# Attention and quantised feed-forward on one core: transposing DMAs ahead of the store, and another tail

## The chip, the cores and the metric

The kernel runs on one core of one Trainium2 chip. The metric is the time of one execution on the device, in microseconds (us); lower is better. Besides the plain runs there is one execution that the hardware profiler recorded; all rows below are from it.

## The reference

For each of 8 batches of 512 rows of 512 numbers, cross attention of the normalised rows over a context, with a dropout mask, a residual, then a feed-forward whose activations are rounded to integers row by row:

```
scores = layernorm(x) @ ctx.T / 0.72
attn   = softmax(scores) * mask
x      = x + (attn @ ctx + bias) @ W
h      = layernorm(x)
scale  = max(|h|) / 127                 (per row, at least 1e-6 / 127)
q      = clip(round(h / scale), -128, 127)
out    = x + (q @ Wq.T) * scale * wscale + ffn_bias
```

## The kernel before

**Tiles.** The 4096 rows are 32 tiles of 128 rows, four to a batch. Per tile TensorE multiplies three times with float32 numbers split in a high and a low part (`product3`, 12 matmuls of 512 columns): context times W (`ctx_times_w`, into ps_vw, a batch ahead), scores (ps_scores), and probabilities times that product (`attend`, ps_attn). `turn_probs` transposes the probabilities (ps_pt) between, and `feed_forward` multiplies the integers, transposed (xq_t), with the weights (ps_ffn, four matmuls in bfloat16).

**Engines.** ScalarE makes the high parts, the exponential, the normalised rows (x_norm), the centred rows (x1_neg) and their rounding to integers (x1_int, in two steps, L840 and L852). VectorE makes the low parts, maxima, statistics, residual (x1) and the output's scaling (`scale_ffn`); it turns blocks of 32x32 of the context (ct_raw) and of the normalised rows (xt_raw), which the DMA has laid out from DRAM (ctx_in; x_blocks from norm_rows, where SyncE stores x_norm first). GpSimd has the rest: context's low part, small factors, and the additions of the bias and of the output.

**Order.** Each engine has a hand-written list: steps d, in a head (tiles 0 to 3), a loop of three rounds of eight steps (tiles 4 to 27), and a tail (28 to 31, base `TAIL` = 28). Engines wait for each other by semaphores only. The code is written for a step `d`: in a step, work for tile d (scores, probabilities), d - 1 (`attend`, residual, centring), d - 2 (feed-forward) and d + 1 to d + 4 (loads, context) stands in a row. SyncE issues every DMA of the kernel, and an issue that waits holds up all that follow it. In a step its list is: context blocks for two tiles (every other step), the four loads of x_blocks for tile d + 1 (`load_rows`), x for d + 4, mask for d + 2, the store of x_norm for d + 2 (`store_rows`), the output's store for d - 4, and the transposing DMA of the integers of tile d - 2 (xq_t<-x_int, L529).

**Tail before.** From tile `BY_PE` = 26 on, TensorE transposes the integers itself (`turn_integers`, ps_ut) and ScalarE copies them (`clear_integers`). In the tail the feed-forward is one step later (d - 3). Tile 31 (`LAST`) is done in halves: `attend_last`, `residual_last`, `aggregate_last`, `round_last` and `finish_last` on VectorE. The probabilities of tile 31 are turned in the middle of tile 30's products (`turn_last_probs`). `warm_up` multiplies ones, with no use for its result.

## Time and profile before

| | us |
|---|---|
| runs shown, median (3 runs) | 328.11 |
| lowest, highest | 327.24, 328.2 |
| the profiled execution | 329.85 |
| its span, first to last instruction | 328.0 |
| TensorE busy in it (matmuls) | 316.8 |
| VectorE busy | 288.8 |
| ScalarE busy | 235.3 |
| GpSimd busy | 223.3 |

The granted clock of TensorE is 0.998 of full over the span. An engine's rows give the start and the length of its work; "[idle before <-releaser]" is how long it had nothing running and what ended that. SPq rows are the times in which SyncE issues a DMA, not the transfer; the transfer's length is "issue to landing". The profile's line numbers are those of the kernel before. A few matmul records are missing in it (a group of "x3" that is four).

### The profile page before, as it was taken

The numbers are of one execution on the slowest core, as the hardware profiler recorded it, in microseconds if no ns is written. First come the engines' busy times: TensorE is split into PE (matmuls) and PEld (weight loads), VectorE is DVE, ScalarE is ACT, GpSimd is POOL, SyncE is SP. The second block draws the span as 40 slices with busy tenths as digits, with TensorE's granted clock in tenths as the row PEclk, the third lists the DMA queues.
The fourth block names the chain that finished last, engine by engine and source line by source line (L and its number), as shares of the span: only waits on it lengthen the run. The fifth ranks groups of instructions, "written<-read, shape, count | busy, mean of one in ns | idle before, by whom it ended". The sixth has DMA issues, their size and how long they took to land.

```text
span 328.0 us, 6024 instructions
## 1 busy us (share of the span) xinstructions
PE 316.8 (97%) x1508; PEld 255.7 (78%) x1524; DVE 288.8 (88%) x568; ACT 235.3 (72%) x440; POOL 223.3 (68%) x359
## 2 busy tenths in 40 slices
PE   8999989998999999999999999999999999999993
PEld 8888868787877777877787887777788878787782
DVE  2887989999898998989999999999999999989986
ACT  4456777787677787768778777877877778766651
POOL 3273677677777676777777778777777877766663
PEclk9999999999999999999999999999999999999999
DMA  7966856657566665757556565655656575433002
GB/s 208 261 237 159 230 144 166 186 155 189 155 188 182 159 194 157 203 155 207 176 145 198 171 198 166 193 177 155 208 155 198 165 209 158 136 104 128 33 32 96
DMA packets 69247, 55.25 MB, mean 168 GB/s; under 512 B 21488, under 2 KB 51952, under 8 KB 69232
## 3 DMA queue, kind: packets, MB, share of 16 engines
q1 hardware_dynamic: 69232, 55.08, 57.9%
q8 instruction: 6, 0.10, 0.1%
q14 instruction: 9, 0.07, 0.1%
HBM read 34.87 MB, written 16.25 MB: 156 GB/s over the span
## 4 chain that ended last, share of the span: by engine, by line
PE 85%; DMA 4%; ACT 3%; DVE 3%; POOL 2%; issue 2%; SPq 0%; POOLq 0%; DVEq 0%; ACTq 0%
PE ps_vw L563 8%; PE ps_vw L565 8%; PE ps_scores L563 8%; PE ps_vw L564 8%; PE ps_scores L565 7%; PE ps_scores L564 7%; PE ps_ffn L724 7%; PE ps_attn L565 7%; PE ps_attn L563 7%; PE ps_attn L564 7%; DMA xq_t<-x_int 4%; PE ps_pt L555 4%; PE ps_ffn L551 1%; ACT x_round L840 1%; PE ps_scores L573 1%
## 5 line engine op out<-in xcount | busy, mean ns | idle before, releaser
L1263 POOL TENSOR_TENSOR ct_lo<-ct_raw,ct_hi 128x512 fp32r<-128x512 f32 x28 | 36.3, 1296 | 24.0 <-ACT ct_hi L774 24.0
L563 PE MATMUL ps_vw<-w_hi,ct_hi 128*128 128x512 f32 x116 | 50.5, 436 | 0.0
L563 PE MATMUL ps_attn<-vw_hi,pt_hi 128*128 128x512 f32 x124 | 48.9, 395 | 0.0
L563 PE MATMUL ps_scores<-ct_hi,xt_hi 128*128 128x512 f32 x124 | 48.5, 391 | 0.0
L565 PE MATMUL ps_attn<-vw_hi,pt_lo 128*128 128x512 f32 x124 | 48.5, 391 | 0.0
L564 PE MATMUL ps_scores<-ct_lo,xt_hi 128*128 128x512 f32 x124 | 48.3, 389 | 0.0
L565 PE MATMUL ps_scores<-ct_hi,xt_lo 128*128 128x512 f32 x124 | 48.2, 389 | 0.0
L564 PE MATMUL ps_attn<-vw_lo,pt_hi 128*128 128x512 f32 x124 | 48.2, 389 | 0.0
L1256 POOL TENSOR_TENSOR out_tile<-ffn_out,x_plus 128x512 f32<-128x512 f32 x31 | 40.3, 1299 | 7.7 <-DVE ffn_out L1010 7.7
L565 PE MATMUL ps_vw<-w_hi,ct_lo 128*128 128x512 f32 x116 | 45.4, 391 | 0.0
L564 PE MATMUL ps_vw<-w_lo,ct_hi 128*128 128x512 f32 x116 | 45.3, 390 | 0.0
L1286 POOL TENSOR_TENSOR x_in<-x_in,bias_w 128x512 f32<-128x512 f32 x32 | 41.5, 1298 | 0.7 <-issue 0.7
L1308 POOL TENSOR_TENSOR x_plus<-x,ffn_bias_wide 128x512 f32<-128x512 f32 x31 | 40.0, 1289 | 0.0
L865 ACT ACTIVATE ps_scores<-ps_scores,neg_max 128x512 f32<-128x512 f32 x32 | 21.2, 662 | 18.4 <-DVE neg_max L1107 18.4
L1273 POOL TENSOR_TENSOR scaled<-x_sum,sum_scale 128x1 f32<-128x1 f32 x27 | 5.6, 206 | 40.5 <-ACT ps_xt L792 40.5
L885 ACT ACTIVATE x_neg<-x,meanvar 128x512 f32<-128x512 f32 x32 | 23.2, 725 | 13.3 <-DVE meanvar L1174 9.6
L946 DVE STREAM_TRANSPOSE xt_raw<-x_blocks 128x512 f32<-128x512 f32 x30 | 32.7, 1089 | 0.0
L724 PE MATMUL ps_ffn<-wq_t,xq_t 128*128 128x512 bf16 x104 | 27.5, 379 | 4.3 <-DMA xq_t<-x_int 2.8
L1107 DVE TENSOR_REDUCE neg_max<-ps_scores 128x1 f32<-128x512 f32 x32 | 22.1, 689 | 10.7 <-PE ps_scores L565 10.4
L946 DVE STREAM_TRANSPOSE ct_raw<-ctx_in 128x512 f32<-128x512 f32 x28 | 30.8, 1100 | 0.0
L809 ACT ACTIVATE vw_hi<-ps_vw 128x512 fp32r<-128x512 f32 x29 | 17.3, 598 | 17.0 <-PE ps_vw L565 17.0
L784 ACT ACTIVATE x_norm<-x_in,norm 128x512 f32<-128x512 f32 x32 | 25.7, 803 | 4.4 <-POOL norm L1236 4.4
(163 smaller groups left out, 778.9 us busy)
## 6 DMA issues: line engine op xcount, KB each, us to landing
x_in<-in_x_dram SPq DMA_DIRECT2D x32, 256.0 KB, 2.8
mask_in<-in_mask_BxSxS_fk_dram SPq DMA_DIRECT2D x32, 256.0 KB, 3.1
out_dram<-out_tile SPq DMA_DIRECT2D x31, 256.0 KB, 2.2
norm_rows<-x_norm SPq DMA_DIRECT2D x30, 256.0 KB, 2.7
x_blocks<-norm_rows SPq DMA_DIRECT2D x120, 64.0 KB, 2.0
ctx_in<-in_ctx_dram SPq DMA_DIRECT2D x56, 128.0 KB, 2.7
ctx_in<-in_ctx_dram SPq DMA_DIRECT2D x4, 256.0 KB, 4.3
x_blocks<-in_L_xattn_weights_dram SPq DMA_DIRECT2D x4, 256.0 KB, 6.5
```

What stands on the lines that cost most here:

```text
L563: nc.tensor.matmul(bank_, lhs_hi(t), rhs_hi(t), start=(t == 0), stop=False)
L564: nc.tensor.matmul(bank_, lhs_hi(t), rhs_lo(t), start=False, stop=False)
L565: last = nc.tensor.matmul(bank_, lhs_lo(t), rhs_hi(t), start=False, stop=(t == NT - 1))
L724: last = nc.tensor.matmul(ffn_bank(base, n)[:, :], xq_t[:, slot(n, 2), t, :], wq_t[:, t, :], start=(t == 0), stop=(t == NT - 1))
L784: nc.scalar.activation(x_norm[:, slot(n, 2), :], x_in[:, slot(n, 8), :], ACT.Identity, bias=norm1[:, k, 1:2], scale=norm1[:, k, 0:1]).then ...
L885: nc.scalar.activation(x1_neg[:, slot(n, 2), :], x1[:, slot(n, 2), :], ACT.Identity, bias=meanvar2[:, slot(n, 4), 0:1], scale=-1.0).then_i ...
L946: nc.vector.transpose(into.rearrange("p t (a i) -> p t a i", a=QUADS), blocks.rearrange("p (a j t) -> p t a j", a=QUADS, t=NT)).then_inc(r ...
L1107: nc.vector.tensor_reduce(col(neg_max, d), ps_scores[:, :], AX_X, ALU.max, negate=True).then_inc(neg_max_ready, 1)
L1256: nc.gpsimd.tensor_tensor(out_tile[:, slot(n, 2), :], ffn_out[:, slot(n, 2), :], x1_plus[:, slot(n, 2), :], ALU.add).then_inc(out_ready, 1)
L1263: nc.gpsimd.tensor_tensor(ct_lo[:, batch_of(n), :, j * P:(j + 1) * P], ct_raw[:, slot(n, 2), :, :], ct_hi[:, batch_of(n), :, j * P:(j + 1) ...
L1286: nc.gpsimd.tensor_tensor(x_in[:, slot(d, 8), :], x_in[:, slot(d, 8), :], bias_w[:, :], ALU.add).then_inc(x_plus_ready, 1)
L1308: nc.gpsimd.tensor_tensor(into, x1[:, slot(n, 2), :], ffn_bias_wide[:, :], ALU.add).then_inc(x1_plus_ready, 1)
```

## The change

**SyncE.** In a step the transposing DMA of tile d - 2 comes right behind its waits, ahead of the output's store; an empty instruction takes the waits. `BY_PE` goes from 26 to 30, so that tiles 26 to 29 are turned by DMA, in the tail's steps 0 to 3, behind the output's store there. Context blocks for tiles 6 and 7 are loaded ahead of the first step; the two broadcast constants are loaded in step 1 instead of step 0.

**TensorE.** No `turn_integers` for tiles 26 to 29. Feed-forward of tile 0 behind the product of context tile 6. Feed-forward of tile 28 behind the products of tile 30 and no longer ahead of them. At the start, the first row tile is transposed one place earlier, and three warm-ups stand where two and two did.

**VectorE, ScalarE, GpSimd.** Context tile 6 is turned and split in steps 0 and 1 and no longer in step 2. In the step of tile 31 VectorE takes the residual of tile 30 first, then the probabilities' low part, then the scaling of tile 28. The mean and variance of tile 30 come from ScalarE's sums (of x1, then of the squares of x1_neg) and small multiplications on GpSimd. `finish_last` does both multiplications ahead of both additions.

```diff
-FILLS = 9
+FILLS = 10
-BETWEEN = 2
+BETWEEN = 3
-BY_PE = TAIL - 2
+BY_PE = TAIL + 2
...
@@ SyncE
             load_mask(1 * P, 1)
+            sp.wait_ge(first_ct_done, PER_BATCH)
+            load_blocks(ctx_in, ctx_flat, (PER_BATCH + 2) * P, PER_BATCH + 2, 2, ctx_loaded)
...
-                if is_tile(base, d, 0):
+                if is_tile(base, d, 1):
                     load_ffn_constants()
...
+                def turn_by_dma(n):
+                    wait_count(sp, x1_int_ready, base, n + 1)
+                    wait_count(sp, ffn_done, base, n - 1)
+                    sp.nop(nofuse=True)
+                    k = slot(n, 2)
+                    sp.dma_start_transpose(xq_t[:, k, :, :], x1_int[:, k, :]).then_inc(xq_t_turned[k], 16)
+
                 if exists(base, d - 2) and not last_batch(base):
-                    wait_count(sp, x1_int_ready, base, d - 2 + 1)
-                    wait_count(sp, ffn_done, base, d - 2 - 1)
+                    turn_by_dma(d - 2)
                 n = d - 4
...
                     sp.dma_start(out_rows[bass.ds(row + n * P, P), :], out_tile[:, k, :]) \
                         .then_inc(out_stored[k], 16)
-                if exists(base, d - 2) and not last_batch(base):
-                    k = slot(d, 2)
-                    sp.dma_start_transpose(xq_t[:, k, :, :], x1_int[:, k, :]).then_inc(xq_t_turned[k], 16)
+                if last_batch(base) and base + d - 2 < BY_PE:
+                    turn_by_dma(d - 2)
...
@@ TensorE
-                if t == PER_BATCH - 1:
+                if t == PER_BATCH - 2:
                     turn_row_tile(0, first_xt_done)
...
-                if t < PER_BATCH - 2:
+                if t == 0:
                     warm_up(ps_ffn, BETWEEN)
...
                 if last_batch(base):
-                    if d > 0 and exists(base, d):
+                    if d > 0 and exists(base, d + 1):
                         feed_forward(d - 3)
                     if exists(base, d - 1):
                         attend(d - 1)
+                    if is_tile(base, d, LAST):
+                        feed_forward(d - 3)
                     if exists(base, d + 1):
                         turn_probs(d)
-                        turn_integers(d - 2)
                     if is_tile(base, d - 1, LAST):
-                        turn_integers(d - 3)
                         feed_forward(d - 3)
                         warm_up(ps_pt, LAST_WARM_UPS)
                         turn_integers(d - 2)
...
-                    if exists(base, d - 2):
+                    if exists(base, d - 2) and not is_tile(base, d - 2, 0):
                         feed_forward(d - 2)
...
+                if is_tile(base, d - 2, 0):
+                    feed_forward(d - 2)
...
@@ ScalarE
                 if is_tile(base, d - 1, LAST):
-                    clear_integers(d - 3)
                     centre(d - 1)
...
-                if late:
-                    clear_integers(d - 2)
...
+                if is_tile(base, d, LAST):
+                    act.wait_ge(x1_ready, LAST)
+                    nc.scalar.activation(ps_xt[:, :], x1[:, slot(d - 1, 2), :], ACT.Identity,
+                                         accum_out=x1_sum[:, 0:1]).then_inc(x1_sum_ready, 1)
                 if exists(base, d - 1) and not is_tile(base, d - 1, LAST):
                     centre(d - 1)
+                if is_tile(base, d, LAST):
+                    act.wait_ge(x1_neg_ready, LAST)
+                    nc.scalar.activation(ps_xt[:, :], x1_neg[:, slot(d - 1, 2), :], ACT.Square,
+                                         accum_out=x1_squares[:, 0:1]).then_inc(x1_squares_ready, 1)
...
@@ VectorE
-                    dve.wait_ge(ut_done, TILES - 2 - BY_PE)
+                    wait_dma(dve, xq_t_turned, TAIL, n - 2)
...
                 def finish_last():
                     n = LAST - TAIL
-                    dve.wait_ge(x1_plus_ready, TILES)
                     for h in range(2):
                         dve.wait_ge(last_ffn_done, h + 1)
...
+                    dve.wait_ge(x1_plus_ready, TILES)
+                    for h in range(2):
                         dve.wait_ge(last_ffn_out_ready, h + 1)
...
+                    if is_tile(base, d, LAST):
+                        split_probs(d)
+                        scale_ffn(d - 3)
+                    else:
+                        wait_count(dve, x1_ready, base, n + 1)
+                        nc.vector.bn_stats(stats2[:, slot(n, 4), :], x1[:, slot(n, 2), :]).then_inc(stats2_ready, 1)
...
+                if is_tile(base, d, 0):
+                    turn_ctx(base, d + 6)
...
@@ GpSimd
+                if is_tile(base, d, LAST):
+                    pool.wait_ge(x1_sum_ready, 1)
+                    nc.gpsimd.tensor_tensor(meanvar2[:, slot(d - 1, 4), 0:1], x1_sum[:, :], mean_scale[:, :],
+                                            ALU.mult).then_inc(meanvar2_ready, 1)
...
+                        pool.wait_ge(x1_squares_ready, 1)
+                        nc.gpsimd.tensor_tensor(x1_var[:, :], x1_squares[:, :], mean_scale[:, :],
+                                                ALU.mult).then_inc(x1_var_ready, 1)
```

The order of instructions at three places follows. A row is an instruction's line, kind, what it writes and reads, its shape and how often it stands in a row; lines of the kernel before and of the changed one differ.

SyncE in the tail before, from the loads of x_blocks for tile 29 on (each x_blocks row is the loads of the next tile; L525 is the output's store):

```order
L441 DMA x_blocks<-norm_rows 32x4x128 x4
L445 DMA mask_in<-in_mask_BxSxS_fk_dram 128x512
L433 DMA norm_rows<-x_norm 128x512
L525 DMA out_dram<-out_tile 128x512
L441 DMA x_blocks<-norm_rows 32x4x128 x4
L445 DMA mask_in<-in_mask_BxSxS_fk_dram 128x512
L433 DMA norm_rows<-x_norm 128x512
L525 DMA out_dram<-out_tile 128x512
L441 DMA x_blocks<-norm_rows 32x4x128 x4
L525 DMA out_dram<-out_tile 128x512 x5
```

The same place of the changed kernel (L453 x_blocks, L544 the output's store, L530 the transposing DMA):

```order
L453 DMA x_blocks<-norm_rows 32x4x128 x4
L457 DMA mask_in<-in_mask_BxSxS_fk_dram 128x512
L445 DMA norm_rows<-x_norm 128x512
L544 DMA out_dram<-out_tile 128x512
L530 DMA_TRANSPOSE xq_t<-x_int 128x4x128
L453 DMA x_blocks<-norm_rows 32x4x128 x4
L457 DMA mask_in<-in_mask_BxSxS_fk_dram 128x512
L445 DMA norm_rows<-x_norm 128x512
L544 DMA out_dram<-out_tile 128x512
L530 DMA_TRANSPOSE xq_t<-x_int 128x4x128
L453 DMA x_blocks<-norm_rows 32x4x128 x4
L544 DMA out_dram<-out_tile 128x512
```

The transposing DMAs of tiles 26 and 27 stand ahead of the loads of x_blocks for tiles 30 and 31.

TensorE in the tail before, end of tile 31's scores and start of tile 30's products:

```order
L565 MATMUL ps_scores<-ct_hi,xt_lo 128x512
L724 MATMUL ps_ffn<-wq_t,xq_t 128x512 x4
L563 MATMUL ps_attn<-vw_hi,pt_hi 128x512
L564 MATMUL ps_attn<-vw_lo,pt_hi 128x512
L565 MATMUL ps_attn<-vw_hi,pt_lo 128x512
```

The changed kernel, second half of tile 30's products, behind the turning of tile 31's probabilities (ps_pt), and start of tile 31's (ps_vw):

```order
L573 MATMUL ps_pt<-identity,probs 128x128 x4
L581 MATMUL ps_attn<-vw_hi,pt_hi 128x512
L582 MATMUL ps_attn<-vw_lo,pt_hi 128x512
L583 MATMUL ps_attn<-vw_hi,pt_lo 128x512
L581 MATMUL ps_attn<-vw_hi,pt_hi 128x512
L582 MATMUL ps_attn<-vw_lo,pt_hi 128x512
L583 MATMUL ps_attn<-vw_hi,pt_lo 128x512
L742 MATMUL ps_ffn<-wq_t,xq_t 128x512 x4
L695 MATMUL ps_vw<-vw_hi,pt_hi 128x256
```

The feed-forward of tile 28 moved from ahead of tile 30's products to between those and tile 31's.

VectorE in the step of tile 31, from its probabilities on, before:

```order
L1129 TENSOR_TENSOR probs<-ps_scores,mask_in 128x512
L1136 RECIPROCAL inv_sum<-prob_sum 128x1
L1010 SCALAR_TENSOR_TENSOR ffn_out<-ps_ffn,x_scale,wscale_wide 128x512
L930 TENSOR_TENSOR pt_lo<-ps_pt,pt_hi 128x512
L1164 SCALAR_TENSOR_TENSOR x<-ps_attn,inv_sum,x_in 128x512
L1169 BN_STATS stats<-x 128x6
L1181 BN_AGGR meanvar<-stats 128x2
```

And changed:

```order
L1157 TENSOR_TENSOR probs<-ps_scores,mask_in 128x512
L1164 RECIPROCAL inv_sum<-prob_sum 128x1
L1190 SCALAR_TENSOR_TENSOR x<-ps_attn,inv_sum,x_in 128x512
L957 TENSOR_TENSOR pt_lo<-ps_pt,pt_hi 128x512
L1037 SCALAR_TENSOR_TENSOR ffn_out<-ps_ffn,x_scale,wscale_wide 128x512
```

The residual of tile 30 comes first, its statistics are gone, and the scaling of tile 28 is last.

## Rows read from the trace of the kernel before

**Rows 1.** The page's first part: busy time (share of the span), instructions of TensorE.

```profile
PE 316.8 (97%) x1508; PEld 255.7 (78%) x1524; DVE 288.8 (88%) x568; ACT 235.3 (72%) x440; POOL 223.3 (68%) x359
```

**Rows 2.** Waits of TensorE: who waited for whom, us in total, times, longest.

```profile
PE ps_ffn L724 <- DMA xq_t<-x_int: 2.8, 4, 1.0
...
PE ps_pt L555 <- DVE probs L1129: 0.4, 1, 0.4
```

**Rows 3.** Timeline of TensorE, first tiles and loop: start, us, work, [idle before, releaser].

```profile
41.69 0.66 PE L555 MATMUL ps_pt<-identity,probs 128*128 128x128 f32 x4 [0.42 <-DVE probs L1129]
42.99 0.81 PE L724 MATMUL ps_ffn<-wq_t,xq_t 128*128 128x512 bf16 x3 [0.65 <-DMA xq_t<-x_int]
...
81.85 0.81 PE L724 MATMUL ps_ffn<-wq_t,xq_t 128*128 128x512 bf16 x3 [0.96 <-DMA xq_t<-x_int]
```

**Rows 4.** Chain that ended last, 75 to 86 us: start, us, what.

```profile
77.40 0.36 SPq L525
...
77.81 3.77 DMA xq_t<-x_int
...
82.90 0.23 PE ps_vw L564
```

**Rows 5.** Issue to landing: norm_rows store at 76.09, output's store at 77.40.

```profile
DMA to landing us min/median/max: 3.6/3.6/3.6
...
DMA to landing us min/median/max: 3.4/3.4/3.4
```

**Rows 6.** Issue to landing of all 26 turning DMAs, then of x_blocks' four at 296.96.

```profile
DMA to landing us min/median/max: 2.4/2.5/3.8
...
DMA to landing us min/median/max: 1.9/2.0/2.0
```

**Rows 7.** Timeline of VectorE in the head, tile 2's step.

```profile
38.39 1.10 DVE L946 STREAM_TRANSPOSE ct_raw<-ctx_in 128x512 f32<-128x512 f32 x1
```

**Rows 8.** Timeline of SyncE's queue, last loop step and tail.

```profile
279.16 1.25 SPq L529 DMA_TRANSPOSE xq_t<-x_int  x1
...
296.96 1.76 SPq L441 DMA_DIRECT2D x_blocks<-norm_rows  x4
```

**Rows 9.** Timeline of ScalarE in the tail: tile 27's integers.

```profile
297.89 0.63 ACT L852 ACTIVATE x_int<-x_round 128x512 bf16<-128x512 f32 x1
```

**Rows 10.** Timeline of VectorE, tail.

```profile
301.02 1.09 DVE L946 STREAM_TRANSPOSE xt_raw<-x_blocks 128x512 f32<-128x512 f32 x1
...
308.42 0.69 DVE L1023 TENSOR_REDUCE abs_max<-x_neg 128x1 f32<-128x512 f32 x1 [0.22 <-ACT x_neg L885]
309.23 0.69 DVE L1107 TENSOR_REDUCE neg_max<-ps_scores 128x1 f32<-128x512 f32 x1
...
316.73 0.47 DVE L1055 SCALAR_TENSOR_TENSOR x<-ps_ct,inv_sum,x_in 128x256 f32<-128x256 f32 x1
```

**Rows 11.** Timeline of TensorE, tail.

```profile
291.81 0.39 PE L555 MATMUL ps_ut<-identity,x_int 128*128 128x128 bf16 x4
...
301.93 1.04 PE L724 MATMUL ps_ffn<-wq_t,xq_t 128*128 128x512 bf16 x4
...
311.51 0.66 PE L555 MATMUL ps_pt<-identity,probs 128*128 128x128 f32 x4
...
316.27 0.40 PE L555 MATMUL ps_ut<-identity,x_int 128*128 128x128 bf16 x4
```

**Rows 12.** Timeline of GpSimd and VectorE at the end: output additions.

```profile
323.38 1.26 POOL L1256 TENSOR_TENSOR out_tile<-ffn_out,x_plus 128x512 f32<-128x512 f32 x1 [0.31 <-DVE ffn_out L1010]
...
323.72 1.20 DVE L1092 TENSOR_TENSOR ct_raw<-ct_raw 128x256 f32<-128x256 f32 x1
...
325.35 0.42 DVE L1092 TENSOR_TENSOR ct_raw<-ct_raw 128x256 f32<-128x256 f32 x1
```

**Rows 13.** ScalarE's sums over a tile by line: busy us, mean ns.

```profile
L798 ACT ACTIVATE ps_xt<-x_in,scaled 128x512 f32<-128x512 f32 x27 | 18.5, 687 | 0.0
```

**Rows 14.** TensorE in the stretch 81 to 82 us: us, busy (instructions), granted clock, DMA share, GB/s.

```profile
81.00:82.00 1.00, 0.15 (x1) 1.00 0.57 135
```

56 lines of the change are left out of this document (35 added, 21 removed).

## Prediction

> **What bounds the kernel now.** Read first the busy times: TensorE works for 316.8 of 328.0 us [rows 1], so only its few idle stretches and its own work are worth anything. Then the waits of TensorE: 2.8 us in four waits for the transposing DMA that turns a tile's integers (xq_t<-x_int), and 0.4 us for the probabilities [rows 2]. The timeline places them [rows 3]: 0.42 and 0.65 us at tile 0's first feed-forward, 0.96 us at 81.85, and two more in the loop that make the rest of the 2.8 (0.69 at 101.51, 0.54 at 140.09). After 145 us the loop has none. The last look goes to the tail (from 281 us), where VectorE has no free time either: its rows follow each other without a gap, so a TensorE that is quicker there meets a VectorE that is not. What lies outside the span (329.85 us of the profiled execution against 328.0) is left as it is.
>
> **The loop: the turning DMA ahead of the store.** SyncE's queue now issues the output's store (0.36 us) between the end of the integers' rounding and the turning DMA [rows 4]. Exchanging them issues the DMA 0.36 us earlier; the added empty instruction that carries the waits costs something under 0.1 us, of which no row tells. The waits that the store needs (the addition on GpSimd) were met earlier in every loop step, so nothing else is held up. Behind the exchange stand the store itself, now 1.25 us later [rows 8], and then the same loads at the same times as before.
> The DMA's landing matters more. Of 26 the median takes 2.5 us and the longest 3.8 [rows 6]; the long ones are those that TensorE waited for. In the long case the queue was full: the store of norm_rows at 76.09 took 3.6 us and landed at 79.7, the output's store at 77.40 took 3.4 and landed at 80.8 [rows 5], the turning DMA landed at 81.57 [rows 4]. They land in turn, 0.8 to 1.1 us apart. Without the output's store in front, the DMA would land about where that did or a little earlier, 80.5. TensorE's wait of 0.96 us ends if it lands before 80.6. So I expect this wait to go, and the two shorter ones by the same sum: together 2.8 less the 0.65 of tile 0, that is 2.2 us, of which I take 2.1. The bounds are 2.2 us and nothing: nothing if the landing hangs on the loads queued before, not on the store.
>
> **The head.** Tile 0's feed-forward moves behind the product of context tile 6 with W (12 products, 2.7 us at the 0.23 us that the chain gives each [rows 4]), which covers its wait of 0.65 us. The transposition of context tile 6 (1.10 us on VectorE [rows 7]) leaves the place ahead of tile 2's maximum for a gap in tile 0's step; what waited 0.42 us for the probabilities [rows 3] had this ahead of it. Its loads move to the start of SyncE's list, where they take the place of the two broadcast constants, as many bytes; the constants go in front of the weights' turning and push the store of norm_rows, and with it the blocks of tile 3, about 1 us later. These land near 39.3 us by my count, when VectorE gets to them about 39.2, so I leave 0.1 us. ScalarE's and GpSimd's halves of the split move with it into idle time. Sum: 0.42 + 0.65 - 0.1 = 1.0 us gained, bounds 0.6 and 1.1. The other order of the first transpositions and warm-ups ends before context tile 3 has come from memory, as now; I take 0, bounds 0.1 either way.
>
> **The tail: what is removed.** TensorE loses four groups of four transpositions (0.39 us busy each [rows 11], some 0.27 us of it on its path), ScalarE four copies, VectorE tile 30's statistics. On TensorE alone that is 0.8 to 1.1 us. I count none of it, since VectorE sets the pace here and the next item makes it later still.
>
> **The tail: what is queued behind the new waits.** SyncE's queue now holds four turning DMAs, each behind a wait for the integers. The one for tile 27 stands ahead of the four loads of x_blocks for tile 31. Before, those started at 296.96 [rows 8]. Tile 27's integers end at 297.89 + 0.63 = 298.52 [rows 9]; the DMA occupies the queue for 1.25 us [rows 8], so the loads start at 299.8. Their fourth starts 1.3 us after the first (1.76 us for four) and lands 2.0 us later [rows 6]: 303.1. VectorE turns these blocks at 301.02 [rows 10], first in its step, ahead of the maximum of tile 30 and all that follows. So VectorE waits: 303.1 - 301.02 = 2.1, of which 0.1 may be won by the step before; I take +2.0 us. Tile 26's DMA stands in the same way ahead of tile 30's blocks, but its integers are ready at the end of the loop, and by the same sum the blocks land ahead of their use; I count nothing.
> From there the rows of VectorE follow without a gap up to tile 31's maximum, which at 309.23 had 0.2 us to spare behind the 0.6 us of the maximum at 308.42 [rows 10]. So the turning of tile 31's probabilities, at 311.51 [rows 11], comes 1.8 us later.
> Next the feed-forward of tile 28. It ran before the products of tile 30, where TensorE would have waited for the probabilities anyway. Now it stands behind them: 0.9 us (1.04 busy, its end overlapped [rows 11]) between those probabilities and the products of tile 31. It was hidden and is now on the path. TensorE ends the products of tile 31, at 316.27 before [rows 11], 1.8 + 0.9 = 2.7 us later. VectorE took them up at 316.73 [rows 10], 0.2 us later than it could have, since it was at tile 30's largest value: +2.5.
> Tile 30's moments by ScalarE cost two sweeps of 0.6 to 0.7 us [rows 13] and some small steps on GpSimd, beside TensorE's products of tile 31. They are hidden unless GpSimd gets to tile 31's variance late; bounds 0 and +0.3, I take 0.
> **The end.** Now VectorE's first addition takes 1.20 us, the second 0.42; GpSimd's addition runs from 323.38 to 324.64 and the long one ends just behind it [rows 12]. With both multiplications first, the time is used: I take -0.3, bounds 0 and -0.5. The Trainium skill, page "SBUF — State Buffer", section "Who interferes with whom", says that a VectorE instruction with two SBUF inputs and a GpSimd one exclude each other, so that the second waits in full; by it the gain would be up to what the multiplication takes, 0.5, and by a fixed first cost it would be 0.
> Sum of the tail: +2.5 - 0.3 = +2.2 us, bounds about 0 and +2.9.
>
> **The sum.** -1.0 - 2.1 + 2.2 = -0.9 us. The profiled execution would go from 329.85 to 328.95. The median of the runs shown is 328.11, 1.7 us below it, and the runs reach from 327.24: some of the waits may be shorter without a profile. I apply the same difference: 327.2 us.
>
> **Rivals.** (1) The wait for tile 31's blocks costs nothing: TensorE and VectorE have room, or the blocks come earlier. For it: until now they land at about 300.3, with room; against it: the order of the queue is fixed and the sum above has no free term. Then the tail is near 0 and the time 328.1 - 3.1 = 325.0 us. (2) Slower: the queue of loads sets the landing, not the store. The price is the whole loop term. It decides at a landing of over 3.4 us for the turning DMAs after the loop's double steps. For it: the store of norm_rows, with no store ahead, took 3.6 us itself [rows 5]. Then -1.0 + 2.2 = +1.2, 329.3 us. (3) TensorE's clock falls in the tail. New idle stretches of some 1.7 us ahead of tile 30's and of tile 31's probabilities stand against the 0.96 us of [rows 3], around which the granted clock stayed at 1.00, the upper level of 2.4 GHz [rows 14]. If it fell to 1.2 GHz, one tile's scores and products, 24 at 0.23 us, would take 5.5 us more: 332.7.
> The Trainium skill, page "TensorE: Matmul & The Clock Gate", section "HAM oscillation — how this bites in real kernels", describes such falls where TensorE waits for loads between short bursts; no row here shows one outside the last 4 us.
> (4) The exchange does nothing because outside the profile there were no waits: then 328.1 - 1.0 + 2.2 = 329.3, which counts with (2).
>
> **How the numbers follow.** Forecast with its own range, 326.2 to 328.4: 0.55. Rival 1: 0.20. Rivals 2 and 4: 0.22. Rival 3: 0.03. A difference within 0.3% (327.1 to 329.1) can't be told from none. The forecast's case lies half on each side of 327.1: 0.27 faster, 0.28 within. Rival 1 is faster (0.20, 0.02 of it near the edge, to within). Rivals 2 and 4 are slower for 0.13, within for 0.09; rival 3 slower. Together faster 0.45, within 0.39, slower 0.16. The range that leaves out two in ten: 324.9 to 329.4.
>
> **What would show it.** Right: in the loop no wait of TensorE for xq_t, and turning DMAs that land in 2.4 to 2.9 us; at tile 0 no 0.65; in the tail a wait of VectorE of about 2 us for x_blocks ahead of the last transposition of blocks, one of TensorE of over 1 us for the probabilities of tiles 30 and 31, x_blocks' last loads some 2.8 us after where they were. Wrong: VectorE goes through that place without a wait (rival 1); landings of 3 us and more and the same waits in the loop (rival 2); a granted clock of half ahead of the last products (rival 3).

## The result, and the profile after

| | before | changed |
|---|---|---|
| median of the runs, us | 328.15 (6 runs) | 331.59 (6 runs) |
| lowest, highest | 327.24, 330.05 | 330.45, 333.0 |
| the profiled execution | 329.85 | 330.45 |
| its span | 328.0 | 328.6 |

The changed kernel is slower: the ratio of the times is 1.0094, with an interval of 1.0064 to 1.0123. Forecast were 327.2 us and at most 329.4. In two later series of the changed kernel the ratio was 1.0114 (1.007 to 1.0159) and 1.0068 (1.0037 to 1.0099). The two profiled executions differ by only 0.6 us: the one of before lies 1.5 to 1.7 us above its kernel's median, the one of after is among the fastest of its kernel. Much of what follows is about that.

The busy times of the changed kernel's page (us, share, instructions) answer to [rows 1]. TensorE works as long as before:

```profile
PE 317.3 (97%) x1506; PEld 254.5 (77%) x1506; DVE 287.3 (87%) x566; ACT 234.8 (71%) x440; POOL 223.3 (68%) x362
```

Its longest waits (us in total, times, longest) answer to [rows 2]. The waits for xq_t went from 2.8 to 0.4 us, and VectorE waits twice for x_blocks, 0.85 us in the head and 2.48 in the tail:

```profile
PE ps_pt L573 <- DVE probs L1157: 3.7, 3, 1.7
DVE xt_raw L973 <- DMA x_blocks<-norm_rows: 3.3, 2, 2.5
```

The timeline of SyncE's queue and of VectorE in the tail (start, us, work, [idle before, releaser]) answers to [rows 8] and [rows 10]. The transposing DMA of tile 27 stands ahead of tile 31's loads. VectorE is done at 298.74 and waits 2.48 us for the last of them:

```profile
296.24 1.20 SPq L530 DMA_TRANSPOSE xq_t<-x_int  x1
297.48 2.00 SPq L453 DMA_DIRECT2D x_blocks<-norm_rows  x4
```

```profile
298.08 0.66 DVE L957 TENSOR_TENSOR pt_lo<-ps_pt,pt_hi 128x512 fp32r<-128x512 f32 x1
301.21 1.10 DVE L973 STREAM_TRANSPOSE xt_raw<-x_blocks 128x512 f32<-128x512 f32 x1 [2.48 <-DMA x_blocks<-norm_rows]
...
313.45 0.75 DVE L1190 SCALAR_TENSOR_TENSOR x<-ps_attn,inv_sum,x_in 128x512 f32<-128x512 f32 x1 [2.07 <-PE ps_attn L583]
...
315.86 0.48 DVE L1082 SCALAR_TENSOR_TENSOR x<-ps_vw,inv_sum,x_in 128x256 f32<-128x256 f32 x1 [0.40 <-PE ps_vw L701]
```

From issue to landing these four loads took (min, median, max; [rows 6] before):

```profile
DMA to landing us min/median/max: 2.0/2.1/2.1
```

The timeline of TensorE in the tail ([rows 11] before) shows who pays. The rows are the probabilities of tiles 28 to 31, the feed-forward of tile 28, and the last group of four products:

```profile
289.20 0.60 PE L573 MATMUL ps_pt<-identity,probs 128*128 128x128 f32 x4
...
296.11 0.60 PE L573 MATMUL ps_pt<-identity,probs 128*128 128x128 f32 x4
...
304.84 0.66 PE L573 MATMUL ps_pt<-identity,probs 128*128 128x128 f32 x4 [1.71 <-DVE probs L1157]
...
311.37 0.66 PE L573 MATMUL ps_pt<-identity,probs 128*128 128x128 f32 x4 [1.38 <-DVE probs L1157]
...
313.26 1.04 PE L742 MATMUL ps_ffn<-wq_t,xq_t 128*128 128x512 bf16 x4
...
323.49 0.60 PE L734 MATMUL ps_xt<-wq_t,xq_t 128*128 128x256 bf16 x4
```

In the same view of the kernel before:

```profile
291.38 0.60 PE L555 MATMUL ps_pt<-identity,probs 128*128 128x128 f32 x4
...
298.48 0.60 PE L555 MATMUL ps_pt<-identity,probs 128*128 128x128 f32 x4
...
305.58 0.60 PE L555 MATMUL ps_pt<-identity,probs 128*128 128x128 f32 x4
...
322.78 0.60 PE L716 MATMUL ps_xt<-wq_t,xq_t 128*128 128x256 bf16 x4
```

From row to row, before against after: tile 28's probabilities to tile 29's 7.10 and 6.91, on to tile 30's 7.10 and 8.73, on to tile 31's 5.93 and 6.53, on to the last group 11.27 and 12.12, from there to the end of the span 5.22 and 5.11. The tail is 36.6 us before and 39.4 after: **2.8 us more**. Up to it, 291.38 became 289.20: **2.2 us less**. That is the 0.6 us between the two spans.

### The profile page after: what moved, and what is told of

Same layout as the page of the kernel before. It is cut to its first block, busy times and chain, and to the rows that moved or that the text cites. A ratio compares the mean times of both kernels' runs of the same rounds, so it can differ in the third digit from the quotient of the medians.

```text
span 328.6 us, 6007 instructions
## 1 busy us (share of the span) xinstructions
PE 317.3 (97%) x1506; PEld 254.5 (77%) x1506; DVE 287.3 (87%) x566; ACT 234.8 (71%) x440; POOL 223.3 (68%) x362
## 4 chain that ended last, share of the span: by engine, by line
PE 68%; DVE 7%; SPq 7%; DMA 7%; POOL 3%; ACT 3%; issue 3%; DVEq 0%; POOLq 0%
PE ps_vw L581 6%; PE ps_vw L583 6%; PE ps_vw L582 6%; PE ps_ffn L742 6%; PE ps_scores L583 6%; PE ps_scores L581 6%; PE ps_scores L582 6%; PE ps_attn L583 6%; PE ps_attn L581 6%; PE ps_attn L582 6%; PE ps_pt L573 3%; DMA x_in<-in_x_dram 2%; SPq L453 2%; DMA norm_rows<-x_norm 2%; SPq L518 2%
## 5 line engine op out<-in xcount | busy, mean ns | idle before, releaser
L1291 POOL TENSOR_TENSOR out_tile<-ffn_out,x_plus 128x512 f32<-128x512 f32 x31 | 40.3, 1301 | 9.5 <-DVE ffn_out L1037 9.5
L742 PE MATMUL ps_ffn<-wq_t,xq_t 128*128 128x512 bf16 x120 | 30.9, 380 | 0.4 <-DMA xq_t<-x_int 0.4
```

What stands on the lines that cost most here:

```text
L742: last = nc.tensor.matmul(ffn_bank(base, n)[:, :], xq_t[:, slot(n, 2), t, :], wq_t[:, t, :], start=(t == 0), stop=(t == NT - 1))
L1291: nc.gpsimd.tensor_tensor(out_tile[:, slot(n, 2), :], ffn_out[:, slot(n, 2), :], x1_plus[:, slot(n, 2), :], ALU.add).then_inc(out_ready, 1)
```

## The experiments

All times are medians; the interval belongs to the ratio to the kernel before, run in turns with it on the same chip. For each trace the table gives two numbers: where tile 28's probabilities are turned (head and loop), and the time from there to the end of the span (tail). "Pairs" are pairs of idle products of ones on TensorE, eight at the end of the changed kernel.

| kernel | runs, us | ratio (interval) | head and loop | tail |
|---|---|---|---|---|
| before | 328.15 | | 291.38 | 36.6 |
| before, second trace | 328.62 (one run) | | 290.20 | 36.6 |
| exchange alone | 328.37 | 0.9993 (0.9968 to 1.0018) | 288.26 | 37.0 |
| head alone | 328.44 | 0.999 (0.9966 to 1.0014) | 289.86 | 36.6 |
| head and exchange | 328.25 | 0.9993 (0.9972 to 1.0014) | 292.02 | 37.0 |
| tail alone | 333.42 | 1.0148 (1.0109 to 1.0186) | 288.83 | 39.3 |
| changed | 331.59 | 1.0094 (1.0064 to 1.0123) | 289.20 | 39.4 |
| changed, second trace | 332.46 | 1.0114 (1.007 to 1.0159) | 287.57 | 42.7 |
| changed, third trace | 331.18 | 1.0068 (1.0037 to 1.0099) | 288.69 | 39.2 |
| tile 26's DMA moved | 332.23 | 1.0094 (1.0064 to 1.0124) | 289.44 | 40.5 |
| one wait filled | 331.59 | 1.0104 (1.0063 to 1.0145) | 288.57 | 40.7 |
| all waits filled | 331.58 | 1.011 (1.0075 to 1.0145) | 288.03 | 40.4 |
| tile 27's DMA moved | 328.23 | 0.9973 (0.9943 to 1.0002) | 290.21 | 36.9 |
| loads first | 327.31 | 0.9975 (0.995 to 1.0) | 287.65 | 37.2 |
| the same, feed-forward ahead | 327.66 | 0.9975 (0.9951 to 0.9999) | 288.65 | 37.1 |
| the same as loads first, 11 pairs | 327.71 | 0.9986 (0.9955 to 1.0017) | 288.61 | 36.8 |
| the same, 4 and 11 pairs | 328.06 | 0.9993 (0.9964 to 1.0023) | 288.27 | 36.8 |
| loads first, constants later | 328.29 | 0.9975 (0.9946 to 1.0005) | 289.37 | 37.8 |
| loads first, old head | 327.86 | 0.9992 (0.9968 to 1.0015) | 288.70 | 38.9 |
| tail alone, loads first | 328.74 | 1.0012 (0.9991 to 1.0033) | 290.65 | 36.9 |

### The three parts apart

**The exchange alone** (the diff's two hunks in SyncE's loop, nothing else):

> The kernel before with one edit: in the head and the loop the transposing DMA is issued ahead of the output's store; the tail turns its integers on TensorE as before. Theory T (the tail costs the time, the exchange is harmless): the trace shows no wait of TensorE for xq_t in the loop or under 0.5 us in sum, and the time is that of before to 2 us less (ratio 0.994 to 1.000), near 1.000 if the ordinary runs of before had no such waits. Rival X (the exchange itself costs in ordinary runs, since the store now collides with the loads behind it): ratio 1.003 to 1.008.

**The head alone:**

> The kernel before with the head's edits alone: earlier loads for context tiles 6 and 7, constants later, context tile 6 turned and split earlier, feed-forward of tile 0 behind the product of context tile 6, order of the first transpositions. Theory T: 0.5 to 1.0 us less than before (ratio 0.997 to 0.9985), the wait of 0.65 us at tile 0 gone. Rival H (the later constants and blocks disturb the first tiles or the loop's loads): ratio 1.001 to 1.005, with waits in the first 60 us that before did not have.

**The tail alone** (the changed kernel with loop and head as before):

> The changed kernel with head and loop as in the kernel before: only the tail's edits are left. Theory T: the tail alone costs 2.2 to 3.4 us (ratio 1.007 to 1.010), VectorE waits 2 to 2.5 us for x_blocks ahead of its last transposition of blocks. Rivals X and H: 1.000 to 1.004.

Neither exchange nor head moves the ordinary time by more than these intervals can tell (the exchange: 1.1 us less to 0.6 more; the head: 1.1 less to 0.5 more). Of the head's theory one sign came true, the wait of 0.65 us is gone in its trace, but so did the sign of its rival: VectorE waits 1.30 us for tile 3's blocks there. The tail alone costs 4.9 us by its ratio (3.6 to 6.1), more than any theory had. In the trace of the exchange alone TensorE waits nowhere for xq_t, as forecast, and still the median stands. So the forecast counted more in the one profiled execution than the runs hold. The second trace of before was made to test that:

> The kernel before once more, unaltered, for a second execution in the trace. The first (329.85 us) had 2.8 us of TensorE's waits for xq_t and was 1.5 us above the median of its own ordinary runs. Theory: those waits belong to some executions only; an execution at 328.4 or below shows one or two of them, 1.3 us or less. Rival: they are in every execution, and what made the first one long lies elsewhere; then 2.5 us or more of them appear again, and the exchange of store and turning DMA should have won over 1 us, which its run (328.37 against 328.39) did not show.

The timeline of TensorE in it has two waits for xq_t, 1.35 us together where the first trace had 2.8, and none in the head:

```profile
100.72 0.81 PE L724 MATMUL ps_ffn<-wq_t,xq_t 128*128 128x512 bf16 x3 [1.04 <-DMA xq_t<-x_int]
...
119.95 0.81 PE L724 MATMUL ps_ffn<-wq_t,xq_t 128*128 128x512 bf16 x3 [0.31 <-DMA xq_t<-x_int]
```

Its 1.35 us is just over the 1.3 of the theory, and its execution (328.62) 0.2 us longer. Over all traces with the store ahead of the turning DMA, the loop's waits for xq_t are 2.19, 1.35, 1.35, 0.93 and 0.39 us, 1.2 in the mean; over the fifteen with the DMA ahead they are 0 in eleven and 0.24, 0.41, 0.53 and 0.75 in four, 0.13 in the mean. By the traces the exchange is worth about 1.1 us, half of what was forecast; that is the edge of what the runs' interval allows. **Head and exchange together:**

> The kernel before with the exchange of store and turning DMA in the loop and the reordered head, and the tail as before. Each of the two alone gave 0.0 us in ordinary runs (328.4). Theory: waits in the loop that one of them removes come back as another's, and together they win what the mended kernel shows: 327.0 to 327.5, that is -1.1 to -1.6; in the trace the turning of tile 28's probabilities stands at 287.6 to 288.7, and from there to the end it is 36.6. Rival: they are worth nothing together as well, 328.2 to 328.6, and the mended kernel's gain of 1.1 lies in its tail.

They win nothing that can be measured with the tail as before; the rival holds for the time. The trace, of the slowest of its twelve runs (330.83), shows by its timeline how the head gives back:

```profile
42.50 1.08 DVE L953 STREAM_TRANSPOSE xt_raw<-x_blocks 128x512 f32<-128x512 f32 x1 [2.83 <-DMA x_blocks<-norm_rows]
...
44.20 0.65 PE L558 MATMUL ps_pt<-identity,probs 128*128 128x128 f32 x4 [2.55 <-DVE probs L1136]
```

VectorE waits 2.83 us for tile 3's blocks, and TensorE 2.55 for the probabilities behind it. With the new head this wait is in eleven of fourteen traces, 0.66 to 2.83 us; with the old head in none of six.

### Which place in the queue costs

**Loads first.** The changed kernel; in the tail each turning DMA goes behind the next step's loads:

```diff
                     load_rows(base, n, row + n * P)
+                if last_batch(base) and d > 0 and base + d - 3 < BY_PE:
+                    turn_by_dma(d - 3)
                 n = d + 4
...
-                if last_batch(base) and base + d - 2 < BY_PE:
-                    turn_by_dma(d - 2)
```

> The changed kernel with one edit: in the tail each transposing DMA is issued behind the next step's four loads of x_blocks and no longer ahead of them. Theory T: the wait of VectorE for x_blocks is gone, TensorE does not wait for tile 30's probabilities, and the time is 1.5 to 2.2 us under the changed kernel's, so ratio to before 1.002 to 1.005. Rivals X and H: nothing is won beyond 0.5 us, ratio 1.008 and up.

It takes back 4.3 us of the change (327.31 against 331.59; by the ratios 1.2%). The timeline of its queue has the loads at 293.25 and the DMA behind them, and TensorE turns tile 30's probabilities without a wait and tile 31's after 1.14 us:

```profile
293.25 1.76 SPq L453 DMA_DIRECT2D x_blocks<-norm_rows  x4
295.12 1.19 SPq L497 DMA_TRANSPOSE xq_t<-x_int  x1
...
301.42 0.60 PE L573 MATMUL ps_pt<-identity,probs 128*128 128x128 f32 x4
...
307.26 0.66 PE L573 MATMUL ps_pt<-identity,probs 128*128 128x128 f32 x4 [1.14 <-DVE probs L1157]
```

**One DMA at a time.** Only tile 27's, or only tile 26's, is moved behind the loads (`base + d - 3 == 27`, `== 26`), the others stay:

> The changed kernel with one of its tail's turning DMAs moved: tile 27's goes behind the four loads for tile 31, the other three stay. Theory that tile 27's place carries the cost: all of the gain of moving them (331.6 to 327.3) comes back, 327.0 to 328.0; VectorE does not wait for x_blocks ahead of the last transposition of blocks. Rival, tile 26's place costs as much in ordinary runs (its DMA stands ahead of tile 30's blocks with some 0.3 us to spare in the trace): only about 2.3 us of 4.3 comes back, 329.3, and a wait for tile 30's blocks is left.

> The changed kernel with only tile 26's turning DMA moved behind the four loads for tile 30; tiles 27, 28 and 29 as in the change. Theory that tile 27's place carries the cost: 331 to 332, no gain, and VectorE's wait of 2.0 to 2.5 us for tile 31's blocks stays. Rival, tile 26's place costs what the trace does not show: 329.3 to 330, that is 1.5 to 2.5 us less than the change. If both this one and the run with only tile 27 moved gain 2 us, the two places share the cost.

Tile 27's place carries all of it: 328.23 against 332.23 on the same chip, where the changed kernel itself took 332.46. In the timeline of the kernel with tile 27's DMA moved the loads start ahead of it, and VectorE turns their blocks without waiting:

```profile
295.80 1.77 SPq L453 DMA_DIRECT2D x_blocks<-norm_rows  x4
297.68 1.19 SPq L497 DMA_TRANSPOSE xq_t<-x_int  x1
...
299.68 1.10 DVE L975 STREAM_TRANSPOSE xt_raw<-x_blocks 128x512 f32<-128x512 f32 x1
```

**The feed-forward of tile 28** back ahead of tile 30's products, with the loads first (in the diff's TensorE part `exists(base, d + 1)` is `exists(base, d)` again, and the two lines for `LAST` go):

> The changed kernel with the tail's turning DMAs behind the next step's loads (the run before this one, 327.31 us), and tile 28's feed-forward back ahead of tile 30's products. Theory of the exposed product: the four products of tile 28 (1.04 us busy, 0.9 on the path) stand between the last probabilities and the products of tile 31; ahead of tile 30's products they fill TensorE's wait for tile 30's probabilities, so the time falls by up to 0.9 us: 326.4. VectorE's scaling of tile 28's result stays where it was and now finds it ready. Rival: with tile 31's blocks on time VectorE no longer makes TensorE wait ahead of tile 30, so the product is 0.9 us of TensorE's work wherever it stands: 327.3, no change. Second rival, to the slow side: TensorE reaches tile 28's product before its turned integers have landed (its DMA is now issued behind the loads) and waits there: 328 or more, with a wait of TensorE for xq_t in the tail.

No gain: the time is the one that the first rival named, but not for its reason. Ahead of tile 30's products the feed-forward does fill a wait: TensorE's for tile 31's probabilities goes from 1.14 us to 0.26. The timeline of TensorE in this trace shows where that is lost again, in tile 31's products:

```profile
311.76 0.74 PE L701 MATMUL ps_vw<-vw_hi,pt_lo 128*128 128x256 f32 x4 [0.48 <-DVE pt_lo L955]
```

VectorE makes the probabilities' low part (pt_lo) late, since in the changed order it stands behind tile 30's residual, for which VectorE waits 2.06 us here. So two things end at nearly the same time there, and taking one away gives 0.13 us.

### Why ordinary runs lose more than the first trace

The first trace has a tail 2.8 us longer; by the runs, tile 27's place alone costs some 4. **The changed kernel again**, twice:

> The changed kernel once more, unaltered, for a second execution in the trace and more times. Its runs so far reach from 330.45 to 333.0, and the traced one is the fastest. Theory of the jittering queue: where a run takes 332 to 333, the landing of tile 31's blocks is later than the 301.2 of the first trace, or a turning DMA takes the queue 2.0 us instead of 1.2, and the wait of VectorE for x_blocks is 3.5 us and more instead of 2.5. Rival: the tail is as in the first trace and the extra time lies before it, in the loop or ahead of the first step: then VectorE's wait for x_blocks is again 2.5 within 0.3, and the turning of tile 28's probabilities is later than 289.2 by what the run is longer. If the traced execution is again a fast one (330.5), nothing is told.

> The changed kernel a third time, unaltered. Both theories of the extra time make a statement on its trace: with a span of 329.5 us and more, either a load for tile 31 lands 3 us or more after its issue (late landings), or the granted clock is 0.50 for some us in the tail with landings of 2.1 us (clock), or both. Tile 28's probabilities are turned at 287.5 to 289.5, and from there to the end it is 39.3 to 42.7 as in the five traces with this tail.

The second trace (332.08 us, close to the median of its series) tells it. Its timeline: head and loop are 1.6 us ahead of the first trace's, the loads for tile 31 are issued 1.6 us earlier, and VectorE still gets them only at 300.94:

```profile
295.87 2.00 SPq L453 DMA_DIRECT2D x_blocks<-norm_rows  x4
...
300.94 1.09 DVE L973 STREAM_TRANSPOSE xt_raw<-x_blocks 128x512 f32<-128x512 f32 x1 [3.83 <-DMA x_blocks<-norm_rows]
...
304.56 1.12 PE L573 MATMUL ps_pt<-identity,probs 128*128 128x128 f32 x4 [3.06 <-DVE probs L1157]
...
308.03 0.63 PE L581 MATMUL ps_scores<-ct_hi,xt_hi 128*128 128x512 f32 x1
308.46 0.63 PE L582 MATMUL ps_scores<-ct_lo,xt_hi 128*128 128x512 f32 x1
...
313.02 0.66 PE L573 MATMUL ps_pt<-identity,probs 128*128 128x128 f32 x4 [0.93 <-DVE probs L1157]
```

Issue to landing of those four loads (min, median, max):

```profile
DMA to landing us min/median/max: 2.0/2.2/3.5
```

One took 3.5 us. And the windows (us, then busy us and instructions of PE, PEld, DVE, ACT, POOL, granted clock, DMA share, GB/s) show two more things:

```profile
300.00:300.40 0.40, 0.40 (x3) 0.34 (x2) 0.00 (x0) 0.00 (x0) 0.00 (x0) 1.00 0.08 12
...
306.00:308.00 2.00, 2.00 (x6) 1.55 (x5) 1.93 (x4) 0.85 (x2) 1.60 (x3) 0.50 0.33 66
...
310.00:312.00 2.00, 2.00 (x8) 1.34 (x7) 1.22 (x5) 0.54 (x1) 0.80 (x1) 0.89 0.00 0
```

From 300.0 on the DMA share is 0.08, near the 0.06 that a single one of sixteen engines gives: it looks as if one were late with its packets while the rest are done; which engine worked was not read. And behind TensorE's 3.06 us without work the granted clock falls to 0.50, the lower level of 1.2 GHz, until past 310; a product of the scores takes 0.43 us instead of 0.23 from row to row, and from tile 30's probabilities to tile 31's it is 8.5 us instead of 6.5. The third trace is like the first (39.2, landings of 2.1, full clock). The trace with tile 26's DMA moved has the fall without the late landing, in its windows and in the timeline of TensorE:

```profile
308.00:310.00 2.00, 2.00 (x6) 1.55 (x5) 1.18 (x2) 0.68 (x1) 1.92 (x3) 0.50 0.36 131
```

```profile
305.05 0.66 PE L575 MATMUL ps_pt<-identity,probs 128*128 128x128 f32 x4 [1.71 <-DVE probs L1159]
```

Here a wait of 1.71 us stands ahead of the fall, as long as the one in the changed kernel's first trace, behind which the clock stayed. From these probabilities to tile 31's it is 7.6 us. **Filling the waits** was to tell the clock's share from the landings':

```diff
+                    if is_tile(base, d + 1, LAST):
+                        wait_count(pe, pt_lo_ready, base, d)
+                        warm_up(ps_pt, 6)
                     if exists(base, d + 1):
                         turn_probs(d)
```

(The idle products write ps_pt, so they wait until VectorE has read tile 29's probabilities from it.)

> The changed kernel with six pairs of idle products of ones on TensorE (1.46 us at the 0.122 us each that the eight pairs in the tail take) ahead of the turning of tile 30's probabilities, where TensorE waits 1.7 us in one trace and 3.1 us in the other. VectorE's wait for x_blocks is not touched. Theory of the clock: in ordinary runs TensorE's granted clock falls to 0.50 behind that wait (303.6 to 310.3 in the second trace, where the scores' products come every 0.43 us instead of 0.23), and the fall is worth some 1.9 us; with the wait filled the clock holds, and the median falls from 331.6 to 332.5 down to about 330.3 (329.8 to 330.8), with the granted clock at 1.00 ahead of tile 31's scores. Rival: the clock is a by-product and the late landings alone make the runs long: 331.6 to 332.5, no change. To the slow side: where the wait is only 1.7 us and the products start late, they delay the turning; 0.2 us more at most.

> The changed kernel with TensorE's three waits in the tail filled with pairs of idle products of ones: eight (1.95 us) ahead of tile 30's probabilities, four (0.98) ahead of tile 31's, eleven instead of eight at the end. VectorE's wait for x_blocks stays. Theory that falls of the clock make part of the loss: no fall in the trace, tail of 39.2 to 40.0 us, and the median about 330.5. Rival, the landings alone: 331.6 as the change, with a wait of VectorE for x_blocks of 3 us and more in the trace. To the slow side: eight pairs can be 0.2 us longer than the shortest wait.

(With all filled: 8 here, 4 in `turn_last_probs`, `LAST_WARM_UPS` = 11.) Neither won anything: 330.3 and 330.5 us, the middle of the forecasts, lie below the intervals, so the clock's theory misses on both at the size that it had. A share of the clock under some 1 us can't be told from none. In the trace with one wait filled the clock is at 1.00 ahead of tile 31's scores, as forecast, but it falls to 0.50 ahead of the last products. In the timeline of the kernel with all filled, the blocks are late again (one load took 3.1 us) and the waits are mostly filled:

```profile
301.03 1.09 DVE L977 STREAM_TRANSPOSE xt_raw<-x_blocks 128x512 f32<-128x512 f32 x1 [3.44 <-DMA x_blocks<-norm_rows]
...
304.63 0.66 PE L573 MATMUL ps_pt<-identity,probs 128*128 128x128 f32 x4 [0.87 <-DVE probs L1161]
```

Its windows show the full clock; here is one of them:

```profile
306.00:308.00 2.00, 2.00 (x11) 1.55 (x9) 1.93 (x4) 0.46 (x1) 1.61 (x3) 1.00 0.33 66
```

Its tail is 40.4 us all the same, 1.0 more than with landings of 2.1. So late landings are enough for an ordinary run; falls of the clock come on top in some, and by the medians they are not what makes most of the loss. The same was tried on the better kernel:

> The changed kernel with the tail's turning DMAs behind the next step's loads (327.31 us; trace 326.64), and eleven instead of eight pairs of idle products at the end, ahead of tile 30's integers: 0.73 us more of the 0.84 us that TensorE waits there. In that kernel's trace the granted clock was 0.67 from 318 to 320 and 0.50 from 320 on, behind two waits of 0.84 and 0.91, and the last twelve products of the feed-forward took 3.4 us against 2.3 in the changed kernel's trace at full clock. Theory of the clock: the last fall goes too, 1.1 us in those executions in which it happens, 0.5 to 1.1 us at the median: 326.2 to 326.8. Rival: the fall happens in few executions, or is caused by the second wait, which stays: 327.3. To the slow side: the added products end behind the integers where these come early, up to 0.3 us.

> As the run before it, with four more pairs of idle products (0.98 us) ahead of the turning of tile 31's probabilities, where TensorE waits 1.1 us in the trace of the kernel with the loads first. Theory: a fall of the clock behind that wait is excluded as well, and the runs between 328 and 330 of that kernel go: median 326.0 to 326.6, with fewer runs over 328. Rival: that wait brings no fall, and in executions where it is short the products delay the turning: 0 to +0.5 us against the run before it.

Both traces keep the full clock up to the last product, and no median falls: the fillings are worth nothing that these intervals can tell. The falls ahead of the last products are real all the same. Of the twelve traces with the new tail and eight pairs, five have one, behind waits of 0.84 to 1.01 us, and their last group starts 2.1 to 2.9 us behind the last transposition instead of 1.5; the three with eleven pairs have none, nor have the five with the old tail.

### What head and tail are worth with the loads first

> The kernel before with the changed tail alone, its turning DMAs behind the next step's loads; head and loop as before. Theory that head and loop carry the mended kernel's gain: 328.4 to 328.9, none; from tile 28's probabilities to the end 36.8 to 37.2 in the trace, against 36.6 before. Rival, the tail carries it: 327.3 to 327.8.

```diff
                     store_rows(base, n, row + n * P)
+                if is_tile(base, d, 1):
+                    load_ffn_constants()
```

(The same two lines are gone from their place ahead of the weights' turning.)

> The changed kernel with the tail's turning DMAs behind the next step's loads (327.3 us; with its near relatives about 0.2% below the kernel before), and the two broadcast constants issued behind step 1's store of norm_rows instead of ahead of the weights' turning. Theory: the store is issued 0.9 us earlier, tile 3's blocks some 0.6 to 1.2 us, VectorE's wait for them near 40 us (0.85 in the change's trace) and TensorE's for the probabilities of tile 1 (0.57) shrink to 0.4 or none: 327.0, that is 0.3 to 0.5 us won. Rival: the constants' own transfers (256 KB each into the tile) now run beside the blocks and hold their landing where it was: 327.4, the wait stays. To the slow side: tile 0's scaling waits for the constants behind everything, over 0.5 us.

> The kernel before with the exchange of store and turning DMA and the changed tail, its turning DMAs behind the next step's loads; the head as before. Theory that the new head gives back at tile 3's blocks what it wins at tile 0's feed-forward: the same time as with the new head within 0.3 us, 327.2 to 327.9, no wait of VectorE for x_blocks in the trace and 0.4 us of TensorE's for the probabilities near 41.5. Rival, the new head is worth its forecast 1.0: 328.3 or more.

The mended tail alone wins nothing (36.9 us in the trace, 36.6 before). With the constants behind the store, tile 3's blocks were issued at 36.33, not earlier, since the turning of the weights itself began late (28.59); VectorE's wait was 0.67: nothing is told of the cause. With the old head there is no such wait, and TensorE's is 0.39, as forecast; the time of 327.86 fits the theory, but the ratio's interval holds the rival's 328.3 as well. In that trace another wait appears: with the loads first, it is the turning DMA that lands late (4.0 us after its issue), and the timeline of TensorE has tile 27's feed-forward wait for it ahead of tile 30's probabilities:

```profile
300.22 1.04 PE L741 MATMUL ps_ffn<-wq_t,xq_t 128*128 128x512 bf16 x4 [1.24 <-DMA xq_t<-x_int]
...
303.84 0.60 PE L572 MATMUL ps_pt<-identity,probs 128*128 128x128 f32 x4
```

No version beats the kernel before by more than 0.3%. The one with the loads first and the new head is at 0.9975 (0.995 to 1.0), its relatives at 0.9975 to 0.9993.

## Why the prediction was wrong

Two steps failed. The waits of one profiled execution were taken off times that did not hold them in full ("I apply the same difference"): that is 2.9 of the 4.4 us between 327.2 and 331.59. And a landing was taken as one number of 2.0 us, with the clock at full: late landings and falls of the clock make most of the other 1.5, which the tail cost more in the mean of seven traces (3.7 against 2.2).

**The wait for tile 31's blocks: right in place and nearly in size.** Forecast was a wait of 2.0 us, with landing 3.3 us after the first issue; the first trace has 2.48 and 3.7, since the four issues took 2.00 us instead of 1.76 and the last landed 2.15 after. Tile 31's probabilities came 22.17 us behind tile 28's instead of 20.13, 2.0 us later (forecast 1.8). Rival 1 is refuted.

**Feed-forward of tile 28: the number fits, and the reason is half of it.** Forecast +0.9, and from tile 31's probabilities to the last group it is 0.85 more. The feed-forward itself puts 0.68 us between the products of tile 30 and of tile 31 (313.26 to 313.94), and the residual of tile 31's first half, which waits for those products, comes 4.49 us behind the probabilities (315.86 - 311.37), before 3.77. That is the forecast's step. But moved back it gave only 0.13 (4.36), since then the low part of the probabilities holds the products up, by 0.48 us in that trace. The forecast had the first limit and not the second, which the new order on VectorE makes. That order was not tried by itself.

**What was removed, put at nothing.** The forecast took none of TensorE's 0.8 to 1.1 us, because VectorE sets the pace. Where the blocks come in time (tile 27's DMA moved) it is 13.78 us from tile 28's probabilities to tile 30's instead of 14.20 before: 0.4 us of it was won.

**The finish: -0.1 instead of -0.3.** The timeline of VectorE and GpSimd, with the changed kernel's last stores, answers to [rows 12]:

```profile
323.92 0.47 DVE L1114 SCALAR_TENSOR_TENSOR ct_raw<-ps_attn,x_scale,wscale_wide 128x256 f32<-128x256 f32 x1
...
324.08 1.26 POOL L1291 TENSOR_TENSOR out_tile<-ffn_out,x_plus 128x512 f32<-128x512 f32 x1 [0.18 <-DVE ffn_out L1037]
324.31 0.47 DVE L1114 SCALAR_TENSOR_TENSOR ct_raw<-ps_xt,x_scale,wscale_wide 128x256 f32<-128x256 f32 x1
324.70 1.26 DVE L1120 TENSOR_TENSOR ct_raw<-ct_raw 128x256 f32<-128x256 f32 x2
...
325.75 0.93 SPq L539 DMA_DIRECT2D out_dram<-ct_raw  x2
```

The stores before:

```profile
325.04 1.09 SPq L520 DMA_DIRECT2D out_dram<-ct_raw  x2
```

The multiplications (0.47 each) now run beside GpSimd's addition, and the two additions behind them take 1.26 together instead of 1.20 + 0.42. From the start of the last group of products VectorE needs 2.47 us instead of 2.99: the 0.5 us is won there. The Trainium skill, page "SBUF — State Buffer", section "Who interferes with whom", has the addition wait for GpSimd's in full. The rows agree: the first addition ends 0.28 us behind GpSimd's in both traces (324.92 against 324.64, and 325.62 against 325.34). What the forecast left out are the stores of tile 31's two halves. Before, the first was issued at 325.04, while VectorE was still at the second half; now both stand behind the long addition, at 325.75 and some 0.45 us later, and the second lands after 2.0 us instead of 1.7. To the end of the span it is 5.11 us instead of 5.22.

**Tail in the trace:** forecast +2.2, measured +2.8, within the bounds. **In ordinary runs** it is more: seven traces with this tail (two of them with filled waits) have 39.2 to 42.7, 40.3 in the mean, 3.7 above before. The step that failed is the landing taken as one number, 2.0 us, from the four loads of tile 31 in one trace [rows 6]. In three of the seven a load took 3.0 to 3.5. The trace of before could have told: its loads of x_blocks land after 3.9 us at the longest between 40 and 60 us, and after 2.8 for tile 30. Before, tile 31's loads landed some 0.7 us ahead of their use (about 300.3 by the prediction's reading, against 301.02) [rows 10]; behind the DMA there is no slack, and a late landing goes to the end. In the thirteen traces in which tile 31's loads do not stand behind a transposing DMA, their landings are all 1.8 to 2.2 us. So the DMA in front may itself be what makes them late; no run here shows how.

**The clock (rival 3)** was given 3 in 100, because the clock had stayed up behind a wait of 0.96 [rows 14]. It fell in the tail of three of the seven. In two it fell ahead of or in tile 31's scores and cost 1.1 and 1.9 us there and not 5.5 (7.6 and 8.5 us from tile 30's probabilities to tile 31's, against 6.5); in the third, with one wait filled, it fell only ahead of the last products and cost 0.8. The Trainium skill, page "TensorE: Matmul & The Clock Gate", section "HAM oscillation — how this bites in real kernels", describes falls of the clock where TensorE waits for loads between bursts of products. The traces agree that such falls exist, behind 3.06 and 1.71 us here. Over the seven they come to 0.5 us in the mean, which the runs with filled waits can't tell from none; that they make most of the loss, those runs speak against.

**The loop: half the size in the traces, and less in the runs.** Forecast -2.1 of 2.2; the traces give 1.1 in the mean, and the runs of the exchange alone at most that. In the first trace of the changed kernel one wait of 0.41 is left (the timeline of SyncE, VectorE and TensorE in head and loop, [rows 3] before):

```profile
33.77 0.58 SPq L445 DMA_DIRECT2D norm_rows<-x_norm  x1
36.04 1.75 SPq L453 DMA_DIRECT2D x_blocks<-norm_rows  x4
...
39.87 1.08 DVE L973 STREAM_TRANSPOSE xt_raw<-x_blocks 128x512 f32<-128x512 f32 x1 [0.85 <-DMA x_blocks<-norm_rows]
...
41.58 0.66 PE L573 MATMUL ps_pt<-identity,probs 128*128 128x128 f32 x4 [0.57 <-DVE probs L1157]
...
99.68 1.04 PE L742 MATMUL ps_ffn<-wq_t,xq_t 128*128 128x512 bf16 x4 [0.41 <-DMA xq_t<-x_int]
```

The landings as a whole hardly moved (median 2.4 instead of 2.5, the longest 3.8 in both), so rival 2 has its part: not every late landing came from the store in front.

**The head: about 0 instead of -1.0.** The wait of 0.65 at tile 0's feed-forward, counted in full, was in two of the six traces with the old head (0.65 and 0.58). And the step "so I leave 0.1 us" failed: the store of norm_rows went from 32.20 to 33.77, the loads of tile 3 from 34.80 to 36.04, later by 1.6 and 1.2 us (forecast about 1), and the rows above have VectorE ready at 39.02 and waiting 0.85. The forecast's 39.3 us for the landing is what 36.0 + 1.3 + 2.0 gives, again with the 2.0 of another place: at this place the slowest of the four loads took 2.8 us before and 2.5 after. TensorE's wait for the probabilities went from 0.42 to 0.57; over the fourteen traces with the new head it is 0.7 in the mean, and 0.4 in all six with the old.

**The sum.** In the trace -2.2 + 2.8 = +0.6 against -0.9; of the 1.5 us between, 0.9 is head and loop and 0.6 the tail. The larger error is the last step: "I apply the same difference". The profiled execution of before was slow for its kernel, by just the waits that the forecast removed; the runs at 328.1 did not hold them in full. Their median already lay 1.7 us below the profiled execution, and the forecast took off both this difference and the waits that are part of it. Rival 4 named this, but priced the tail at 2.2 where runs pay 2 to 5. Taken together, -0.2 (head and exchange in the runs) and +3.7 (mean tail) give 331.7, and 331.59 was measured. That this fits so closely is luck: the tail alone cost 4.9 us in the runs, and the changed kernel 3.1, 3.7 and 2.2 in its three series.

**Left open:** why some landings are late in some executions; and why head and exchange, which in the traces bring tile 28's probabilities some 1.4 us forward (290.3 in the mean of the four with neither, 288.9 of the thirteen with both), show no more than 0.2 us in the runs with the old tail (interval -0.9 to +0.5), but more with a new one: from the tail alone to the changed kernel the ratio falls from 1.0148 to 1.0094, and with the loads first from 1.0012 to 0.9975, that is 1.8 and 1.2 us, each just clear of its noise.

## What to carry to other kernels

A queue that issues in order makes every added issue a delay of all behind it: ask for the first one behind whose data an engine takes up at once, and put the new issue behind that one. Slack between a landing and its use covers late landings; price a cut of it with the longest landing of such transfers in the trace (3.9 us here), not with the median (2.0). A wait seen in one profiled execution that lies above the median of the runs is worth its mean over several traces. And when one instruction is moved off the path and nothing is won, look for the second one that ends just behind it before its cost is called nothing.
